# A new order of all engines and PSUM banks in the third stage of a decoder kernel: value projections between the head products and the scores

## The chip, the cores and the metric

The kernel runs on one core of one Trainium2 chip. The metric is the device time of the whole program in microseconds, as the median of several executions. Numbers of the trace come from one further execution under the hardware profiler.

## The reference

The input is 64 sequences of 64 tokens with 128 features. Three stages follow each other, each with a residual addition: a self-attention, a cross-attention, and a stack of six layers, which the change touches. Cut to what matters, one of the six layers is:

```python
qkv = shift_tokens(x) @ Wqkv[i]                 # 128 -> 3 * 1024, 16 heads of 64
q, k = l2norm(q) * q_scale[i], l2norm(k) * k_scale[i]
q, k = rotary(q), rotary(k)                     # k with the inverse scale
sim = where(mask, -max, (q @ k.T) * 8.0)        # local window, causal
out = softmax(sim) @ v
x = out @ Wo[i] + x
xn = layernorm(shift_tokens(x)) * g + b
a, gate = split(xn @ W1[i] + b1[i])             # 2 * 341
x = a * gelu(gate) @ W2[i] + b2[i] + x
```

All of it is float32.

## The kernel before

A tile holds two sequences, 128 tokens on 128 partitions, so there are 32 tiles a layer and N = 192 tiles in six layers. The third stage is the function `local`. Every engine runs its own program, written out as one loop over i from 0 to N + LAST (LAST = 8), and in each pass it takes one step of each kind for tiles of different age: `queries(i, 0)` of the newest tile, `scores(i - 1)` of the one before, `ff_out(i - 8)` of the oldest. The order of the calls in the five loops, and which of the eight PSUM banks each result uses, are written out in the program; nothing reorders them at run time. An engine executes its own list strictly in that order. Between engines there are counting semaphores: `Counted` translates "this half of tile t is done" into a count, from the order in which the halves are written, and `wait_ge` holds the engine until the count is there. A bank is used by several results in turn, so some waits are only there to keep a bank from being overwritten too early.

What a tile goes through, with the lines under which the profile shows it:

- TensorE: `input_turned` (a transpose, `ident,ystat`, L1008), `queries` and `keys` (products with the weights WA, L1032), `queries_turned` and `keys_turned` (four transposes each of R, L1008), `values` (eight products, L1083), `scores` (mask L1098, 64 small products L1103), `probs_turned` (transposes of P, L1008), `head_outputs` (64 small products of V and PT, L1144), `out_projection` (L1160), `normal_turned` (transpose of xn), `ff_in` (L1128), `ff_out` (L1024).
- ScalarE: squares of queries and keys from their banks (L1219), copies out of the banks (L1194), exponentials (L1232), the normalised tile (L1242), and the gates.
- VectorE: rotation of queries and keys from the banks into R (L1319), sums of squares, a seed for the inverse root (L1344), the maximum of the scores and its subtraction, sums of rows and their inverse (L1373), the two additions to Y (L1294 attention, L1300 feed-forward), the gating.
- GpSimd: `queries_added` and `keys_added` are DMAs from R to R that add the second half of the rotation (L1419 and L1424, issued from GpSimd's queue), `inverse_lengths` is twelve short steps (L1465 to L1472), `keys_scaled` (L1432), `scores_scaled` (L1438), `probs_scaled` (L1444), `inverse_deviation` (L1450 to L1454). `keys_scaled` waits for the landing of the keys' DMA, and by the order of the loop everything below it waits too.
- SyncE issues the loads: the tile's shifted input, the shifted tile for the feed-forward part, and the weights of the next layer.

R, which the rotation writes and the DMAs, the scaling and the transposes read, exists once for queries and once for keys; P, qT, kT and PT exist twice.

GpSimd's loop before is this one:

```python
for i in range(N + LAST + 1):
    queries_added(i)
    probs_scaled(i - 3, 0)
    keys_added(i)
    inverse_lengths(i)
    keys_scaled(i, 0)
    keys_scaled(i, 1)
    scores_scaled(i - 1, 1)
    probs_scaled(i - 2, 1)
    scores_scaled(i - 1, 0)
    inverse_deviation(i - 4)
```

## Time and profile before

| | |
|---|---|
| median of three executions | 3528.43 us (3526.76 to 3532.59) |
| the profiled execution | 3525.89 us, its span 3524.1 us |
| granted TensorE clock | 0.993 of full speed |
| TensorE products | 3377.9 us busy, 96% of the span, 49,605 of them |
| TensorE weight loads | 2495.3 us, 71%, 49,605 of them |
| VectorE | 2811.5 us, 80% |
| ScalarE | 2792.7 us, 79% |
| GpSimd | 2475.5 us, 70% |
| the chain that ended last | TensorE 78% of the span, "issue" 2%, each other engine at most 1% |

Busy time counts how long an engine's instructions ran, overlapping ones once. A busy TensorE is not one at its peak. "issue" in the chain or in a wait is time in which the engine waited for nothing that the profile shows. The third stage begins near 566 us, and its 192 tiles enter between 569.4 and 3446.0 us.

### The profile page before, as it was taken

To read this page: it belongs to the slowest core of one execution; us is meant where nothing else is said; L and a number is where in the kernel's file an instruction comes from. 1 tells how busy PE (TensorE), PEld (TensorE's weight loads), DVE (VectorE), ACT (ScalarE), POOL (GpSimd) and SP (SyncE) were. 2 spreads that over 40 slices of the span, in tenths; PEclk is the share of its full clock that TensorE was granted. 3 is DMA by queue.
4 is the path that set the end of the run, shared out by engine and by line. 5 is a ranking of instruction groups with operands and counts; after the bars stand their busy time and mean duration, and the time that the engine had idled before them with its cause. 6 is when DMAs were issued, how large, how long until landed. Compare 5 with 4: busy or idle time off the path is not lost.

```text
span 3524.1 us, 120975 instructions
## 1 busy us (share of the span) xinstructions
PE 3377.9 (96%) x49605; PEld 2495.3 (71%) x49605; DVE 2811.5 (80%) x5297; ACT 2792.7 (79%) x5522; POOL 2475.5 (70%) x4812
## 2 busy tenths in 40 slices
PE   8989997999999999999999999999999999999997
PEld 5778774677777777777777777777777777777776
DVE  6834445888888888888888888888888888888885
ACT  5756664688888888888888888888888888888885
POOL 5622224777777777777777777777777777777774
PEclk9999998999999999999999999999999999999999
DMA  3000002444444444444444444444444444444441
GB/s 101 3 10 8 9 6 50 92 82 82 82 81 89 95 82 82 80 88 97 82 82 82 83 90 93 82 82 80 90 96 83 82 82 88 78 85 83 88 85 39
DMA packets 200382, 260.17 MB, mean 74 GB/s; under 512 B 123161, under 2 KB 145438, under 8 KB 199838
## 3 DMA queue, kind: packets, MB, share of 16 engines
q0 software_dynamic: 55296, 201.35, 30.4%
q1 hardware_dynamic: 143820, 50.88, 5.8%
q8 instruction: 400, 6.55, 0.8%
q14 instruction: 144, 1.18, 0.1%
q10 hardware_dynamic: 722, 0.21, 0.0%
HBM read 23.95 MB, written 2.10 MB: 7 GB/s over the span
## 4 chain that ended last, share of the span: by engine, by line
PE 78%; issue 2%; DVE 1%; POOL 1%; DMA 1%; ACT 0%; SPq 0%; POOLq 0%; DVEq 0%
PE bank L1032 18%; PE bank L1008 16%; PE bank L1083 10%; PE bank L1160 10%; PE bank L1128 7%; PE bank L1144 6%; PE bank L1103 5%; PE bank L1024 3%; PE bank L1098 2%; DVE R L1319 1%; DMA R<-R 1%; POOL R L1432 0%; POOL P L1444 0%; DVE ss L1332 0%; POOL P L1438 0%
## 5 line engine op out<-in xcount | busy, mean ns | idle before, releaser
L1319 DVE TENSOR_TENSOR R<-bank,tables 128x1024 f32<-128x1024 f32 x768 | 903.6, 1218 | 167.5 <-ACT sq L1219 127.4
L1032 PE MATMUL bank<-WA,xcT 128*128 128x512 f32 x1536 | 757.6, 596 | 1.8 <-ACT xcT L1194 1.8
L1008 PEld LDWEIGHTS bank<-ident,R 128*128 128x128 f32 x3072 | 371.6, 141 | 307.0 <-issue 299.9
L1444 POOL TENSOR_TENSOR P<-P,inv_sum 128x512 f32<-128x512 f32 x384 | 458.2, 1193 | 13.1 <-DVE inv_sum L1373 12.1
L1332 DVE TENSOR_REDUCE ss<-sq 128x16 f32<-128x1024 f32 x384 | 460.3, 1199 | 0.0
L1219 ACT ACTIVATE sq<-bank 128x512 f32<-128x512 f32 x768 | 438.2, 595 | 23.9 <-PE bank L1032 23.5
L1432 POOL TENSOR_TENSOR R<-R,rn 128x512 f32<-128x512 f32 x384 | 392.3, 1042 | 88.1 <-DMA R<-R 73.4
L1008 PE MATMUL bank<-ident,R 128*128 128x128 f32 x3072 | 429.8, 273 | 3.3 <-POOL R L1432 2.4
L1438 POOL TENSOR_TENSOR P<-P,rn 128x512 f32<-128x512 f32 x384 | 402.5, 1048 | 2.1 <-DVE P L1361 2.1
L1160 PE MATMUL bank<-WO,OT 128*128 128x128 f32 x3072 | 386.4, 279 | 1.7 <-ACT OT L1194 1.7
L1083 PE MATMUL bank<-WV,xcT 128*64 128x512 f32 x1536 | 376.0, 606 | 3.2 <-DVE R L1319 2.9
L1160 PEld LDWEIGHTS bank<-WO,OT 128*128 128x128 f32 x3072 | 357.4, 192 | 5.3 <-ACT OT L1194 1.9
L1194 ACT ACTIVATE PT<-bank 128x512 f32<-128x512 f32 x384 | 230.2, 599 | 146.8 <-PE bank L1008 146.8
L1194 ACT ACTIVATE kT<-bank 128x512 f32<-128x512 f32 x384 | 233.3, 608 | 133.6 <-PE bank L1008 133.6
L1032 PEld LDWEIGHTS bank<-WA,xcT 128*128 128x128 f32 x1536 | 248.6, 192 | 97.2 <-issue 94.3
L1128 PE MATMUL bank<-xnT,W 128*128 128x128 f32 (+1 forms) x2304 | 287.5, 275 | 0.0
L1194 ACT ACTIVATE V<-bank 128x512 f32<-128x512 f32 x384 | 230.5, 600 | 71.9 <-PE bank L1083 71.9
L1008 PEld LDWEIGHTS bank<-ident,P 128*128 128x128 f32 x1536 | 170.8, 141 | 164.1 <-issue 155.1
L1103 PE MATMUL bank<-kT,qT 64*64 64x64 f32 x12288 | 234.5, 219 | 54.6 <-issue 54.6
L1103 PEld LDWEIGHTS bank<-kT,qT 64*64 64x64 f32 x12288 | 229.7, 135 | 71.0 <-issue 61.9
L1361 DVE TENSOR_TENSOR P<-bank,mx 128x512 f32<-128x512 f32 x384 | 263.2, 686 | 6.7
L1128 PEld LDWEIGHTS bank<-xnT,W 128*128 128x128 f32 (+1 forms) x2304 | 264.8, 180 | 0.1
(154 smaller groups left out, 7082.5 us busy)
## 6 DMA issues: line engine op xcount, KB each, us to landing
R<-R POOLq DMA_DIRECT2D x384, 512.0 KB, 5.3
WA<-in_wqkv SPq DMA_DIRECT2D x24, 256.0 KB, 2.8
ystat<-Y SPq DMA_DIRECT2D x192, 32.0 KB
ystat<-Y SPq DMA_DIRECT2D x384, 15.8 KB
ys<-Y SPq DMA_DIRECT2D x192, 32.0 KB
ys<-Y SPq DMA_DIRECT2D x384, 15.8 KB
WV<-in_wqkv SPq DMA_DIRECT2D x6, 512.0 KB, 5.9
WO<-in_wo SPq DMA_DIRECT2D x6, 512.0 KB, 4.3
```

Source lines behind the costliest of these rows:

```text
L1008: return nc.tensor.transpose(dst, src, m.ident[:, :])
L1032: mm(b[QK_BANK[n, half]][:, :], m.xsT[:, t % 2, :], cols[:, half, :, :], start=True, stop=True)\
L1083: last = mm(V_BANK[bb][64 * e:64 * e + 64, :], m.xsT[:, t % 2, bb * 64:bb * 64 + 64], cols[:, e, :, :], start=True, stop=True)
L1103: last = mm(S_BANK[a][64 * bb:64 * bb + 64, hp * 64:(hp + 1) * 64], m.qT[head, t % 2, at:at + 64], m.kT[head, t % 2, at:at + 64], start=Fa ...
L1128: last = mm(FF_BANK[c][0:rows, side * 128:(side + 1) * 128], m.W1[:, off + at:off + at + rows], m.xnT[:, t % 2, :], start=True, stop=True)
L1160: last = mm(OUT[:, 0:128], m.OT[:, t % 2, at:at + 128], wo[:, c * 128:(c + 1) * 128], start=(c == 0), stop=(c == PAIRS - 1))
L1194: return nc.scalar.activation(dst, src, ACT.Copy)
L1219: nc.scalar.activation(by_half[:, half, :, :], b[QK_BANK[n, half]][:, :].rearrange("p (h d) -> p h d", d=32), ACT.Square)\
L1319: tt(both, src.unsqueeze(1).to_broadcast([128, 2, 16, 32]), tab.unsqueeze(2).to_broadcast([128, 2, 16, 32]), ALU.mult).then_inc(s.rotated. ...
L1332: nc.vector.tensor_reduce(m.ss[:, t % 2, 16 * n:16 * n + 16], m.sq[:, n, :].rearrange("p (h d) -> p h d", d=HD), AX.X, ALU.add)\
L1438: tt(part, part, wide(m.rn[:, t % 4, a:16:2]), ALU.mult).then_inc(s.scaled.sem, 1)
L1444: tt(part, part, wide(m.inv_sum[:, t % 2, 8 * a:8 * a + 8]), ALU.mult).then_inc(s.normal.sem, 1)
```

## The change

The instructions and what they compute stay the same; each engine's list of calls within a pass, the banks, and the waits that go with them are new.

- TensorE: `values` of tile i moves from behind `scores` to between `head_outputs` and `scores`. The two `queries` products now follow each other, the transposes of queries, the transpose of xn (a pass later than before) and `ff_out` follow them, and the transposes of keys and of the probabilities' half 1 stand between and behind the two `keys` products.
- ScalarE: the same calls in a new order; the first exponential stands among the squares, `normal_out` and `normalised` work on tiles one pass older.
- VectorE: the rotation of keys takes half 1 first; maximum and subtraction alternate; `statistics` stands near the end of the pass, and `ff_added` last, for the tile i - 7 in place of i - 8 at the second place.
- GpSimd: `probs_scaled` of half 0 moves from between the two DMAs (tile i - 3) to behind `keys_scaled` (tile i - 2); the scalings of keys, half 1 first, are no longer next to each other; `inverse_deviation` is for a tile one pass older.
- Banks: all have new numbers but those that happen to agree.
- Waits: each step waits for what frees its new bank. New on TensorE: `queries(t, 0)` for the subtraction of the scores' half 0, `queries_turned` for that of half 1, `keys(t, 1)` for the feed-forward addition, `values` for the copy of the turned keys, `head_outputs` for the rotation of the queries' half 1, `probs_turned` for the rotation of keys and the copy of queries, `scores` for the copy of the head outputs.

The diff, cut: most unchanged lines are left out, and those of the five loops stand.

```diff
--- before.py
+++ after.py
@@ -898,11 +898,11 @@
-    QK_BANK = {(QUERIES, 0): 3, (QUERIES, 1): 6, (KEYS, 0): 1, (KEYS, 1): 2}
-    TURNED_IN, TURNED_OUT = b[4], b[6]
-    KT_BANK, QT_BANK, V_BANK = (b[7], b[0]), (b[7], b[4]), (b[1], b[4])
-    S_BANK, PT_BANK, PV_BANK = (b[5], b[6]), (b[0], b[0]), (b[4], b[3])
-    OUT, FF_BANK, FF_OUT = b[0], (b[2], b[1], b[7]), b[5]
+    QK_BANK = {(QUERIES, 0): 1, (QUERIES, 1): 2, (KEYS, 0): 4, (KEYS, 1): 6}
+    TURNED_IN, TURNED_OUT = b[2], b[7]
+    KT_BANK, QT_BANK, V_BANK = (b[0], b[5]), (b[3], b[0]), (b[0], b[5])
+    S_BANK, PT_BANK, PV_BANK = (b[1], b[3]), (b[4], b[3]), (b[1], b[2])
+    OUT, FF_BANK, FF_OUT = b[7], (b[0], b[5], b[6]), b[6]
@@ -911,15 +911,15 @@
-    s.qk, s.squared, s.rotated = counted("qk", *four), counted("squared", *four), counted("rotated", *four)
+    s.qk, s.squared, s.rotated = counted("qk", *four), counted("squared", *four), counted("rotated", (QUERIES, 0), (QUERIES, 1), (KEYS, 1), (KEYS, 0))
...
-    s.q_added, s.k_added, s.k_scaled = sem("local_q_added"), sem("local_k_added"), counted("k_scaled", 0, 1)
+    s.q_added, s.k_added, s.k_scaled = sem("local_q_added"), sem("local_k_added"), counted("k_scaled", 1, 0)
...
-    s.q_turned, s.q_copied = counted("q_turned", 1, 0), counted("q_copied", 0, 1)
+    s.q_turned, s.q_copied = counted("q_turned", 0, 1), counted("q_copied", 0, 1)
...
-    s.scores, s.mx, s.less = sem("local_scores"), counted("mx", 0, 1), counted("less", 1, 0)
-    s.scaled, s.probs, s.row_sum = counted("scaled", 1, 0), counted("probs", 0, 1), counted("row_sum", 0, 1)
-    s.inverse, s.normal = counted("inverse", 0, 1), counted("normal", 1, 0)
+    s.scores, s.mx, s.less = sem("local_scores"), counted("mx", 0, 1), counted("less", 0, 1)
+    s.scaled, s.probs, s.row_sum = counted("scaled", 0, 1), counted("probs", 0, 1), counted("row_sum", 1, 0)
+    s.inverse, s.normal = counted("inverse", 1, 0), counted("normal", 1, 0)
@@ -1010,7 +1010,9 @@
-                    at_least(pe, s.v_copied.sem, s.v_copied.upto(1, t))
+                    at_least(pe, s.o_copied.sem, s.o_copied.upto(1, t - 4))
+                    if t < 5:
+                        at_least(pe, s.rotated.sem, s.rotated.upto((QUERIES, 1), t))
@@ -1037,23 +1039,22 @@
-                    else:
-                        at_least(pe, s.less.sem, s.less.upto(1, t - 1))
+                        at_least(pe, s.less.sem, s.less.upto(0, t - 1))
...
-                    if half == 1 and t < 2:
-                        at_least(pe, s.rotated.sem, s.rotated.upto((KEYS, 1), t))
+                    if half == 1:
+                        at_least(pe, s.y, t - 7)
+                    elif t < 2:
+                        at_least(pe, s.rotated.sem, s.rotated.upto((KEYS, 0), t))
...
-                        pe.wait_ge(s.q_copied.sem, s.q_copied.upto(0, t + 1))
-                    elif t < 8:
-                        at_least(pe, s.y1, t - 3)
+                        pe.wait_ge(s.q_copied.sem, s.q_copied.upto(1, t + 1))
@@ -1063,9 +1064,9 @@
+                        at_least(pe, s.less.sem, s.less.upto(1, t))
+                    else:
...
-                    elif t == N - 1:
-                        pe.wait_ge(s.v_copied.sem, s.v_copied.upto(1, t + 1))
@@ -1075,10 +1076,8 @@
-                        pe.wait_ge(s.rotated.sem, s.rotated.upto((KEYS, 0), t + 1))
+                        at_least(pe, s.k_copied.sem, s.k_copied.upto(0, t))
...
-                    else:
-                        at_least(pe, s.o_copied.sem, s.o_copied.upto(0, t - 3))
@@ -1088,10 +1087,10 @@
-                    at_least(pe, s.xn_copied, t - 4)
-                    at_least(pe, s.y, t - 6)
-                    if t < 6:
-                        pe.wait_ge(s.rotated.sem, s.rotated.upto((QUERIES, 1), t + 2))
+                    at_least(pe, s.o_copied.sem, s.o_copied.upto(0, t - 2))
+                    if t < 5:
+                        pe.wait_ge(s.rotated.sem, s.rotated.upto((QUERIES, 0), t + 2))
+                        at_least(pe, s.p_copied.sem, s.p_copied.upto(1, t - 1))
@@ -1109,9 +1108,9 @@
-                        pe.wait_ge(s.p_copied.sem, s.p_copied.upto(1, t + 1))
+                        pe.wait_ge(s.rotated.sem, s.rotated.upto((KEYS, 0), min(t + 4, N)))
...
-                        pe.wait_ge(s.k_copied.sem, s.k_copied.upto(1, min(t + 3, N)))
+                        pe.wait_ge(s.q_copied.sem, s.q_copied.upto(0, min(t + 3, N)))
@@ -1121,8 +1120,9 @@
-                    pe.wait_ge(s.v_copied.sem, s.v_copied.upto(0, min(t + 8, N)))
-                    pe.wait_ge(s.rotated.sem, s.rotated.upto((KEYS, 1), min(t + 8, N)))
+                    pe.wait_ge(s.v_copied.sem, s.v_copied.upto(1, min(t + 8, N)))
+                    if t >= N - 8:
+                        pe.wait_ge(s.y, t)
@@ -1132,10 +1132,8 @@
-                    pe.wait_ge(s.v_copied.sem, s.v_copied.upto(0, t + 1))
-                    pe.wait_ge(s.q_copied.sem, s.q_copied.upto(1, min(t + 4, N)))
-                    if t < 2:
-                        pe.wait_ge(s.rotated.sem, s.rotated.upto((QUERIES, 0), t + 5))
+                    pe.wait_ge(s.v_copied.sem, s.v_copied.upto(1, t + 1))
+                    pe.wait_ge(s.rotated.sem, s.rotated.upto((QUERIES, 1), min(t + 5, N)))
@@ -1149,11 +1147,8 @@
-                    pe.wait_ge(s.o_copied.sem, s.o_copied.upto(0, t + 1))
...
-                    if t >= N - 6:
-                        pe.wait_ge(s.p_copied.sem, s.p_copied.upto(0, min(t + 2, N)))
@@ -1164,27 +1159,27 @@
             def normal_turned(t):
                 if exists(t):
                     pe.wait_ge(s.xn, t + 1)
-                    pe.wait_ge(s.rotated.sem, s.rotated.upto((QUERIES, 1), min(t + 7, N)))
+                    pe.wait_ge(s.y1, min(t + 3, N))
                     turned(TURNED_OUT[:, 0:128], m.xn[:, t % 2, :]).then_inc(s.xn_turned, 1)
 
             for i in range(N + LAST + 1):
                 input_turned(i)
                 out_projection(i - 5)
                 queries(i, 0)
-                queries_turned(i - 1, 1)
                 queries(i, 1)
                 queries_turned(i - 1, 0)
+                queries_turned(i - 1, 1)
+                normal_turned(i - 7)
+                ff_out(i - 8)
                 keys(i, 0)
+                keys_turned(i - 1, 1)
+                probs_turned(i - 3, 1)
                 keys(i, 1)
-                keys_turned(i - 1, 1)
                 keys_turned(i - 1, 0)
-                ff_out(i - 8)
-                probs_turned(i - 3, 1)
-                normal_turned(i - 6)
                 head_outputs(i - 4)
-                scores(i - 1)
                 values(i, 0)
                 values(i, 1)
+                scores(i - 1)
                 probs_turned(i - 3, 0)
                 ff_in(i - 7)
 
@@ -1265,23 +1260,23 @@
                 input_out(i)
                 gates(i - 8)
                 squares(i, QUERIES, 0)
+                queries_out(i - 1, 0)
                 squares(i, QUERIES, 1)
-                queries_out(i - 1, 0)
+                exponents(i - 2, 0)
                 squares(i, KEYS, 0)
+                queries_out(i - 1, 1)
                 keys_out(i - 1, 1)
-                queries_out(i - 1, 1)
                 squares(i, KEYS, 1)
                 keys_out(i - 1, 0)
-                normal_out(i - 6)
-                exponents(i - 2, 0)
+                normal_out(i - 7)
+                probs_out(i - 3, 1)
                 outputs_out(i - 4, 0)
-                probs_out(i - 3, 1)
+                values_out(i, 0)
+                normalised(i - 6)
+                values_out(i, 1)
+                outputs_out(i - 4, 1)
                 exponents(i - 2, 1)
-                normalised(i - 5)
-                outputs_out(i - 4, 1)
-                values_out(i, 0)
                 probs_out(i - 3, 0)
-                values_out(i, 1)
 
         @block.vector
         def _(dve):
@@ -1307,11 +1302,10 @@
-                    if half == 0:
-                        if n == QUERIES:
-                            at_least(dve, s.q_turned.sem, s.q_turned.upto(0, t))
-                        elif t < 9:
-                            at_least(dve, s.k_turned.sem, s.k_turned.upto(0, t))
+                    if n == KEYS and half == 1:
+                        at_least(dve, s.k_turned.sem, s.k_turned.upto(0, t))
+                    elif n == QUERIES and half == 0 and t < 9:
+                        at_least(dve, s.q_turned.sem, s.q_turned.upto(1, t))
@@ -1385,23 +1379,23 @@
             for i in range(N + LAST + 1):
                 rotary(i, QUERIES, 0)
                 rotary(i, QUERIES, 1)
-                statistics(i - 5)
                 squares_summed(i, QUERIES)
-                ff_added(i - 8)
+                rotary(i, KEYS, 1)
                 rotary(i, KEYS, 0)
-                rotary(i, KEYS, 1)
                 squares_summed(i, KEYS)
                 seeded(i)
                 maximum(i - 1, 0)
+                less_maximum(i - 1, 0)
+                row_sums(i - 2, 1)
+                row_sums(i - 2, 0)
                 maximum(i - 1, 1)
                 less_maximum(i - 1, 1)
-                row_sums(i - 2, 0)
-                less_maximum(i - 1, 0)
+                inverse_sums(i - 2, 1)
+                gated(i - 7)
+                attention_added(i - 4)
+                statistics(i - 5)
                 inverse_sums(i - 2, 0)
-                attention_added(i - 4)
-                gated(i - 7)
-                row_sums(i - 2, 1)
-                inverse_sums(i - 2, 1)
+                ff_added(i - 7)
 
         @block.gpsimd
         def _(pool):
@@ -1420,12 +1414,12 @@
-                    pool.wait_ge(s.rotated.sem, s.rotated.upto((KEYS, 1), t + 1))
+                    pool.wait_ge(s.rotated.sem, s.rotated.upto((KEYS, 0), t + 1))
...
-                    if j == 0:
+                    if j == 1:
@@ -1474,15 +1468,15 @@
 
             for i in range(N + LAST + 1):
                 queries_added(i)
-                probs_scaled(i - 3, 0)
                 keys_added(i)
                 inverse_lengths(i)
+                keys_scaled(i, 1)
+                scores_scaled(i - 1, 0)
+                probs_scaled(i - 2, 1)
                 keys_scaled(i, 0)
-                keys_scaled(i, 1)
+                probs_scaled(i - 2, 0)
                 scores_scaled(i - 1, 1)
-                probs_scaled(i - 2, 1)
-                scores_scaled(i - 1, 0)
-                inverse_deviation(i - 4)
+                inverse_deviation(i - 5)
 
 
 # ---- launch: one core; inputs and outputs as the reference has them ----

```

## Rows read from the trace of the kernel before

**Rows 1.** Groups of instructions, 709 to 3430 us: name, shapes, count | busy us, mean ns | idle before.
```profile
L1008 PE MATMUL bank<-ident,ystat 128*128 128x128 f32 x180 | 53.9, 300 | 0.0
```
**Rows 2.** TensorE in order of time, one undisturbed cycle: start us, us, line, operation, count.
```profile
2057.91 0.30 PE L1008 MATMUL bank<-ident,ystat 128*128 128x128 f32 x1
...
2065.75 0.60 PE L1008 MATMUL bank<-ident,P 128*128 128x128 f32 x4
2066.19 0.27 PE L1008 MATMUL bank<-ident,xn 128*128 128x128 f32 x1
2066.40 1.16 PE L1144 MATMUL bank<-PT,V 64*64 64x64 f32 x64
2067.51 0.41 PE L1098 MATMUL bank<-causalb,identb 64*64 64x512 bf16 x4
2067.72 1.13 PE L1103 MATMUL bank<-kT,qT 64*64 64x64 f32 x64
2068.78 1.94 PE L1083 MATMUL bank<-WV,xcT 128*64 128x512 f32 x8
2070.65 0.66 PE L1008 MATMUL bank<-ident,P 128*128 128x128 f32 x4
...
2072.57 0.30 PE L1008 MATMUL bank<-ident,ystat 128*128 128x128 f32 x1
```
**Rows 3.** Who waited for whom, 709 to 3430 us: us in total, times, longest.
```profile
POOL R L1432 <- DMA R<-R: 68.2, 99, 2.8
...
PE bank L1103 <- issue: 53.0, 58, 1.5
...
POOL P L1444 <- DVE inv_sum L1373: 2.2, 8, 0.5
```
**Rows 4.** The chain that ended last, around one gap: start us, us, what.
```profile
2089.38 0.86 PE bank L1032 x2
2090.24 0.44 PE bank L1008 x4
...
2097.24 0.43 PE bank L1103 x26
2097.66 0.97 issue
```
**Rows 5.** The page's DMA queues: packets, MB, share of 16 engines.
```profile
q8 instruction: 400, 6.55, 0.8%
```
**Rows 6.** GpSimd in order of time, three cycles; what ended an idle time in brackets.
```profile
1310.45 0.94 POOL L1419 DMA_DIRECT2D R<-R  x1
1311.12 1.35 POOL L1444 TENSOR_TENSOR P<-P,inv_sum 128x512 f32<-128x512 f32 x1
1313.04 0.88 POOL L1424 DMA_DIRECT2D R<-R  x1 [0.56 <-DVE R L1319]
...
1319.26 2.04 POOL L1432 TENSOR_TENSOR R<-R,rn 128x512 f32<-128x512 f32 x2 [0.89 <-DMA R<-R]
1321.26 1.05 POOL L1438 TENSOR_TENSOR P<-P,rn 128x512 f32<-128x512 f32 x1
1322.26 1.04 POOL L1444 TENSOR_TENSOR P<-P,inv_sum 128x512 f32<-128x512 f32 x1
1323.26 1.05 POOL L1438 TENSOR_TENSOR P<-P,rn 128x512 f32<-128x512 f32 x1
...
1325.59 0.94 POOL L1419 DMA_DIRECT2D R<-R  x1
...
1327.69 0.88 POOL L1424 DMA_DIRECT2D R<-R  x1
...
1334.31 2.04 POOL L1432 TENSOR_TENSOR R<-R,rn 128x512 f32<-128x512 f32 x2 [1.29 <-DMA R<-R]
...
1340.64 0.94 POOL L1419 DMA_DIRECT2D R<-R  x1
...
1348.07 2.04 POOL L1432 TENSOR_TENSOR R<-R,rn 128x512 f32<-128x512 f32 x2 [0.27 <-DMA R<-R]
```
**Rows 7.** VectorE in order of time, feed-forward addition and the rotations behind it.
```profile
2066.55 0.28 DVE L1300 TENSOR_TENSOR Y<-Y,bank 128x128 f32<-128x128 f32 x1
2066.75 2.35 DVE L1319 TENSOR_TENSOR R<-bank,tables 128x1024 f32<-128x1024 f32 x2
```
**Rows 8.** Tile R with GpSimd's instructions, 709 to 3430 us: its DMAs, issue to landing.
```profile
DMA to landing us min/median/max: 4.5/5.3/8.0
```

## Prediction

> **What bounds the kernel now.** I read the page first: TensorE is busy 96% of the span, VectorE and ScalarE some 80%, GpSimd 70%, so only TensorE looks like a bound. Then I asked how even the third stage runs. The transpose of an input tile, one in each pass of the loop, stands 180 times in 2,721 us, which is 15.12 us a cycle [rows 1]. An undisturbed cycle takes 2072.57 - 2057.91 = 14.66 us on TensorE, with no gap in it [rows 2]. So 0.46 us a cycle is lost. The list of waits names the larger part: TensorE waits inside the scores (L1103) for "issue", that is for nothing that the profile shows, 58 times, 53.0 us in all [rows 3]. The chain shows one of them: 26 products, 0.97 us of nothing, then the rest [rows 4]. With these waits TensorE executes the two densest runs of the program back to back: 64 head products from 2066.40, the mask at 2067.51, 64 products of the scores until 2068.78, some 270 instructions in 2.4 us [rows 2]. The instruction queue of the page brought 400 packets, 6.55 MB, 16 KB each [rows 5]; at 64 bytes an instruction that is 102,400, near the 99,210 products and loads of TensorE on the page and its waits. One packet then feeds 256 instructions, fewer than the two runs together hold. I take the gap for a late packet.
>
> The Trainium skill speaks against this reading (Runtime: NRT & Kernel Launch, section Instruction fetch mechanics): refills come in blocks of 256 instructions, and the cost of crossing into a new one is mostly hidden by the issue floor. The block size agrees with the packets here, "mostly hidden" doesn't agree with 53.0 us. By that rule the spreading would gain nothing.
>
> The last view is GpSimd alone, in order of time, and it decides my forecast. In each cycle GpSimd issues an accumulating DMA for the queries (L1419), one for the keys (L1424), computes the inverse lengths, and must then wait until the keys' DMA has landed before it scales the keys (L1432); it waited for that in 99 of 180 cycles [rows 3]. After that point come two scalings of keys, three steps on the probabilities and the inverse deviation, then the next queries' DMA. In the cycle from 1310.45: the queries' DMA is issued at 1310.45, scaling of keys begins at 1319.26 after a wait, the next queries' DMA is issued at 1325.59 [rows 6]. That is a closed loop on one engine in order: 8.81 us for the two transfers, 6.33 us of work. The next loops measure 1334.31 - 1325.59 = 8.72 and again 6.33, so 15.1 us each, already more than TensorE's 14.66; others are shorter and the slack between the engines evens it out. The keys' transfer gains nothing from an earlier issue: issued 2.59 us behind the queries' it took 6.22, issued 2.10 behind it took 6.62, as if it stood behind the first [rows 6].
>
> **The change part by part.**
>
> TensorE's order. The same instructions run. The eight products of values (1.87 us, 2068.78 to 2070.65 [rows 2]) now stand between head products and scores. 132 pairs within 2.4 us become two runs of at most 1.3 us with 1.87 us of slow work between them. If my reading of the gap is right it closes: the gap was 0.97 us [rows 4], on average 53.0/58 = 0.91, and 1.87 us more are available. Worth up to 53 us if TensorE is the bound, nothing if it isn't. Lower bound nothing (the gap only moves).
>
> The array changes its tiling once more: full to quarter to column tiles to quarter to full. A change costs here 0.10 us: the single transpose ahead of the head products takes 0.21 us (2066.19 to 2066.40), a transpose within its run 0.44/4 = 0.11 [rows 2]. One more is +0.1 us a cycle, 19 us if TensorE binds; but the head products no longer run straight into the mask, where the rows can't tell how much of 1.11 us was a join. I take 0, between -0.1 and +0.1. The Trainium skill (TensorEngine Tiling (Array Packing), section Key Properties) says that a change of tiling mode drains the array; by it the upper end would be taken, 14.76 us.
>
> Banks and waits. New waits on TensorE: queries and their transposes on the subtracted scores, keys half 1 on the feed-forward sum, head products on the queries' rotation, values on the copied keys. Behind each stands all of TensorE. The tightest that I find is that of the head products on the rotation of the newest queries. Between feed-forward product and head products TensorE has both key products (0.86 us each) and three groups of four transposes (0.44 each [rows 4]), 3.04 us. In that time VectorE, whose list ends with the feed-forward addition and begins anew with the queries, has the addition, 0.20 us to the next start, and two rotations, 2.35 us [rows 7]: 2.55, and 0.5 to spare less the signals. I take 0, and up to 0.2 us a cycle if it is late.
>
> VectorE and ScalarE. No instruction is added or dropped. VectorE is busy 80% of the span by the page, so the new wait for the feed-forward product at the end of its pass has some 2 us of idle time to lie in; queued behind it are the next rotations, counted above. Statistics and normalisation come a pass later, and `LAST` stays 8: nothing in the steady part.
>
> GpSimd's order. This is the term that counts. The normalisation of the probabilities' half 0 stood between the two DMA issues (1311.12 [rows 6]), beside the transfers, where GpSimd would have waited anyway. It now stands behind the keys' landing with the other five. Between scaling and the next queries' DMA there are now six steps and the deviation, 6.33 us plus one step. That step measures 1323.26 - 1322.26 = 1.00 us where no DMA is written beside it [rows 6]. So 7.33 us. A wait inside it I leave out: for the inverse sums it waited 2.2 us in 180 cycles [rows 3], and both are now formed before the pass in which they are used ends. That makes 7.33 a lower bound of this part.
>
> The two transfers remain. From the queries' issue to the keys' scaling the sample has 8.81, 8.72, and 7.43 (1348.07 - 1340.64) us [rows 6]. Over 180 cycles the median landing is 5.3 us behind an issue, least 4.5, most 8.0 [rows 8]; with 2.59 us between the issues and 0.07 to start, 7.96. I take 8.1, nearer to the median of all than to the three. The ends are 7.43 and 8.8.
>
> **The sum.** GpSimd's loop becomes 8.1 + 7.33 = 15.43 us, above TensorE's 14.66 and above today's mean of 15.12. It binds every cycle, since queries' DMA, landing and steps follow each other on one engine, and nothing can run ahead of it. +0.31 us a cycle, from about the fifth tile to the last of 192, 187 cycles: +58 us. TensorE's closed gap is worth nothing then: it idles some 0.8 us a cycle ahead of the transposes of probabilities or keys. Filling and draining I take as unchanged: the drain has the same chain per tile, up to 5 us either way. The profiled execution took 3525.9 us (span 3524.1 and 1.8 around it), the median of the runs is 2.5 us above it. 3528.4 + 58 = 3586.
>
> **The rivals.**
> - **TensorE stays the bound and the gap closes** (faster). The loop on GpSimd would have to be short: 7.43 + 7.33 = 14.76 us, which needs every pair of transfers at the sample's best. A cycle of 14.8 gives (14.8 - 15.12) x 187 = -60 us: 3469. For it: if packets of instructions are what delays the transfers, their new times may miss them. Against it: the two other loops of the sample take 8.7 and more. It decides below 7.79 us of landing (7.79 + 7.33 = 15.12). Chance 0.15.
> - **Break-even.** Landing 7.75 to 7.83 us, the gain eaten exactly: 3522 to 3535, 3528. Chance 0.10.
> - **Worse than the forecast.** Both DMAs are issued closer together and the transfers meet more of other traffic, 8.8 us as in the sample: 16.13 us a cycle, +189 us. Partly so, 8.5 us: +133 us, 3661. Chance 0.10.
> - **The gap doesn't close**, since it has another cause. Then it lies in TensorE's new idle time, and the time is the forecast's. That is part of the forecast.
>
> **How the numbers follow.** Forecast 0.65, with 7.9 to 8.4 us of landing: 15.23 to 15.73, +21 to +114 us, 3549 to 3642. The range reaches down to break-even and some way into the faster rival, 3510, and up to 3642. Within 0.2% (7 us, about what a measurement of this kernel can tell from no change): 0.10. Faster: 0.15. Slower: 0.65 + 0.10 = 0.75.
>
> **What would show it.** Right: GpSimd waits for the keys' DMA in nearly all cycles, 0.5 us and more each; 7.3 us from that scaling to the next queries' DMA in every cycle, without a wait; TensorE idle ahead of the transposes of probabilities, released by GpSimd; the row "L1103 <- issue" nearly gone. Wrong: a cycle on TensorE of 14.7 without gaps, which would mean that the transfers land within 7.4 us of the queries' issue; or TensorE waiting for VectorE's rotation ahead of the head products, which would mean that my placing of VectorE was off.

## The result and the profile after

The changed kernel takes 3649.35 us (median of four runs, 3645.76 to 3653.86), beside 3530.51 us for the kernel before on the same chip: a ratio of 1.0333, 95% interval 1.0317 to 1.0348. It is slower by 119 us; 58 were forecast. The profiled execution took 3645.8 us, against 3525.9 before, so the traces carry the whole difference.

The page of the changed kernel: busy time of each engine, the chain that ended last, and two groups of instructions (busy, mean ns of one, idle before them and its releaser). Lines are numbered anew: the DMAs are L1413 (queries) and L1418 (keys), scaling of keys L1426, scores' products L1102.

```profile
PE 3358.6 (92%) x49605; PEld 2446.6 (67%) x49605; DVE 2827.0 (78%) x5297; ACT 2824.3 (78%) x5522; POOL 2466.6 (68%) x4812
...
DMA 39%; POOL 38%; PE 3%; DVE 2%; issue 2%; ACT 0%; SPq 0%; DVEq 0%; POOLq 0%
...
L1426 POOL TENSOR_TENSOR R<-R,rn 128x512 f32<-128x512 f32 x384 | 400.4, 1043 | 453.3 <-DMA R<-R 452.9
...
L1008 PE MATMUL bank<-ident,P 128*128 128x128 f32 x1536 | 252.7, 287 | 195.6 <-POOL P L1438 195.1
```

TensorE is still the busiest engine, 92%, and yet it has 3% of the chain. The chain goes round a loop: GpSimd, the DMAs R<-R, GpSimd again. Busy shares don't show such a bound; the chain does.

The list of waits of the changed kernel in 712 to 3556 us, the even part of the stage (us in total, times, longest):

```profile
POOL R L1426 <- DMA R<-R: 433.7, 180, 4.8
...
PEld bank L1008 <- POOL P L1438: 224.2, 179, 1.6
...
PE bank L1008 <- POOL P L1438: 182.0, 161, 1.4
```

Beside [rows 3]: GpSimd's wait for the keys' DMA was 68.2 us in 99 cycles and is now 433.7 in 180. The scores' products no longer wait for "issue" (53.0 us before, no such row for TensorE now). In its place TensorE waits for the normalised probabilities, 182.0 us.

GpSimd in order of time through one loop (start, duration, line; the twelve short steps in between left out):

```profile
2020.23 0.94 POOL L1413 DMA_DIRECT2D R<-R  x1
2020.88 1.19 POOL L1418 DMA_DIRECT2D R<-R  x1
...
2029.06 1.04 POOL L1426 TENSOR_TENSOR R<-R,rn 128x512 f32<-128x512 f32 x1 [2.88 <-DMA R<-R]
2030.06 1.05 POOL L1432 TENSOR_TENSOR P<-P,rn 128x512 f32<-128x512 f32 x1
2031.06 1.04 POOL L1438 TENSOR_TENSOR P<-P,inv_sum 128x512 f32<-128x512 f32 x1
...
2036.38 0.94 POOL L1413 DMA_DIRECT2D R<-R  x1
```

From the keys' scaling to the next queries' issue it takes 2036.38 - 2029.06 = 7.32 us: the forecast's 7.33. From the queries' issue to the scaling it takes 2029.06 - 2020.23 = 8.83 us. Taken over the 180 cycles of the trace, tile 10 to 189: 7.35 us of work, and 8.43 us to the scaling (8.36 to the keys' landing, 0.07 to start), where 8.1 was forecast. The sum is 15.78 us, the mean cycle.

So the loop was forecast and the loop is there. What was missed is 0.33 us of landing, 60 us in all. In the trace of before the same stretch has a mean of 8.03 us to landing. It isn't one value with a small spread. In the changed kernel 114 of 182 cycles have 8.4 to 8.8 us, 28 less than 7.6, and only 3 lie between 8.0 and 8.4; before, they spread from 7.3 to 8.8, with 57 below 7.6 and 46 from 8.4 to 8.8. The experiments ask what decides between short and long.

### The profile page after: what moved, and what is told of

Read it like the earlier page. It is cut to its first block, busy times and chain, and to the rows that moved or that the text cites. A ratio compares the mean times of both kernels' runs of the same rounds, so it can differ in the third digit from the quotient of the medians.

```text
span 3644.0 us, 120785 instructions
## 1 busy us (share of the span) xinstructions
PE 3358.6 (92%) x49605; PEld 2446.6 (67%) x49605; DVE 2827.0 (78%) x5297; ACT 2824.3 (78%) x5522; POOL 2466.6 (68%) x4812
## 4 chain that ended last, share of the span: by engine, by line
DMA 39%; POOL 38%; PE 3%; DVE 2%; issue 2%; ACT 0%; SPq 0%; DVEq 0%; POOLq 0%
DMA R<-R 39%; POOL R L1426 10%; POOL P L1432 10%; POOL P L1438 10%; POOL R L1413 3%; POOL rstd L1446 3%; POOL nmr L1448 1%; DVE R L1313 1%; POOL vare L1444 1%; PE bank L1034 1%; PE bank L1008 1%; PE bank L1128 0%; PE bank L1155 0%; DVE ss L1326 0%; PE bank L1026 0%
## 5 line engine op out<-in xcount | busy, mean ns | idle before, releaser
L1426 POOL TENSOR_TENSOR R<-R,rn 128x512 f32<-128x512 f32 x384 | 400.4, 1043 | 453.3 <-DMA R<-R 452.9
L1008 PEld LDWEIGHTS bank<-ident,R 128*128 128x128 f32 x3072 | 362.3, 141 | 341.0 <-issue 174.7
L1214 ACT ACTIVATE sq<-bank 128x512 f32<-128x512 f32 x768 | 452.2, 589 | 111.3 <-PE bank L1034 110.5
L1008 PE MATMUL bank<-ident,P 128*128 128x128 f32 x1536 | 252.7, 287 | 195.6 <-POOL P L1438 195.1
L1438 POOL TENSOR_TENSOR P<-P,inv_sum 128x512 f32<-128x512 f32 x384 | 400.6, 1043 | 6.3 <-DVE inv_sum L1367 6.3
L1227 ACT ACTIVATE P<-P 128x512 f32<-128x512 f32 x384 | 243.5, 634 | 205.6 <-POOL P L1432 205.2
L1155 PE MATMUL bank<-WO,OT 128*128 128x128 f32 x3072 | 374.7, 276 | 0.6 <-ACT OT L1189 0.5
L1008 PEld LDWEIGHTS bank<-ident,P 128*128 128x128 f32 x1536 | 161.6, 141 | 252.5 <-POOL P L1438 239.6
L1295 DVE TENSOR_TENSOR Y<-Y,bank 128x128 f32<-128x128 f32 x192 | 55.3, 288 | 298.3 <-PE bank L1026 298.3
L1347 DVE TENSOR_REDUCE mx<-bank 128x8 f32<-128x512 f32 x384 | 263.4, 686 | 7.3 <-PE bank L1102 7.1
```

The costliest lines, as they stand in the source:

```text
L1008: return nc.tensor.transpose(dst, src, m.ident[:, :])
L1155: last = mm(OUT[:, 0:128], m.OT[:, t % 2, at:at + 128], wo[:, c * 128:(c + 1) * 128], start=(c == 0), stop=(c == PAIRS - 1))
L1214: nc.scalar.activation(by_half[:, half, :, :], b[QK_BANK[n, half]][:, :].rearrange("p (h d) -> p h d", d=32), ACT.Square)\
L1426: tt(part, part, wide(m.rn[:, t % 4, 16 + 8 * j:24 + 8 * j]), ALU.mult).then_inc(s.k_scaled.sem, 1)
L1438: tt(part, part, wide(m.inv_sum[:, t % 2, 8 * a:8 * a + 8]), ALU.mult).then_inc(s.normal.sem, 1)
```

## The experiments

### Undoing GpSimd's part, and making it alone

```diff
                 queries_added(i)
+                probs_scaled(i - 3, 0)
                 keys_added(i)
...
                 keys_scaled(i, 0)
-                probs_scaled(i - 2, 0)
```

> The changed kernel with one line of it undone: GpSimd's normalisation of the probabilities' half 0 stands again between the two DMA issues, one pass later, as before the change. TensorE, VectorE, ScalarE and all banks stay as changed. Theory (GpSimd's closed loop sets the time): the work between the landing of the keys' DMA and the next queries' DMA falls from 7.33 to 6.33 us, the landing stays near 8.1 to 8.4, so the loop takes 14.4 to 14.8 us and TensorE's 14.6 becomes the bound again; with the gap in the scores closed the time falls below the kernel before: 3445 to 3480 us. Rival 1 (the new orders of TensorE, VectorE or the banks lose the time): stays at 3640 to 3650. Rival 2 (the landing grows to 8.8 once the step lies between the issues, as some cycles of the kernel before show): 15.1 us a cycle, about 3530, the kernel before again.

3494.6 us (3489.4 to 3503.7), ratio to before 0.9909 (0.9893 to 0.9925). One moved step is worth 155 us; rival 1 falls, and rival 2 would have needed 8.8 us of landing and 3530 us. But it isn't at TensorE's bound either: chain and waits (712 to 3380 us) of this kernel are

```profile
POOL 32%; DMA 29%; PE 15%; DVE 5%; issue 2%; ACT 0%; SPq 0%; POOLq 0%; DVEq 0%
...
POOL R L1426 <- DMA R<-R: 250.1, 173, 4.5
```

The work is 6.35 us, as it should be, but the keys land 8.54 us behind the queries' issue: 14.97 us a cycle. The expectation was low by 15 us or more, for the same reason as the forecast: the landing was taken from another kernel. The kernel is faster than the one before although its landing is the longest so far.

The other way round, the kernel before with GpSimd's part alone:

```diff
                 queries_added(i)
-                probs_scaled(i - 3, 0)
                 keys_added(i)
...
                 scores_scaled(i - 1, 0)
+                probs_scaled(i - 2, 0)
                 inverse_deviation(i - 4)
```

> The kernel before with GpSimd's part of the change alone: the normalisation of the probabilities' half 0 leaves its place between the two DMA issues and goes, a pass earlier, behind the scaling of the scores' half 0 at the end of the order. Theory (GpSimd's loop): 7.33 us of work behind the keys' landing; with a landing of 8.1 us, as forecast, 15.43 us a cycle and 3586 us; with 8.43, as the changed kernel shows, 15.76 us and 3645. Which of the two it is tells whether the longer landing comes with the two issues standing closer together (then it is here too) or with something else of the change. Rival (the loop isn't the bound): 3530 and below, no change.

3551.0 us (3540.2 to 3558.1), ratio 1.0073 (1.0056 to 1.0089). Neither value: 7.35 us of work as expected, but a landing of 7.77 us, 15.20 a cycle. Here too the issues stand 0.67 us apart in 76 of 182 cycles, and in these the landing has the same mean as in the others, 7.75 and 7.78 us; the shortest ones got shorter, 7.18 us instead of 7.35. That the issues stand close together therefore doesn't lengthen the landing. The two halves of the change make a square:

| | GpSimd's order before | GpSimd's order changed |
|---|---|---|
| all else before | landing 8.03, 3528 us | 7.77, 3551 us (+23) |
| all else changed | 8.54, 3495 us (-34) | 8.36, 3649 us (+119) |

The parts alone come to -11 us, together to +119. And the landing follows the other engines' orders, in both columns: it is longer by half a microsecond where they run their new ones, though the DMAs and their data are the same.

### The two transfers in a row

```diff
-pool.dma_start(m.R[:, QUERIES, 0, :], m.R[:, QUERIES, 1, :], accum_op=ALU.add)
+pool.dma_start(m.R[:, QUERIES, 0, 0:512], m.R[:, QUERIES, 1, 0:512], accum_op=ALU.add)
```

> The changed kernel with the queries' accumulating DMA cut to half of its columns (the rotated halves of the other queries aren't added, so the output is wrong). Theory (the two transfers go one after the other and stand in GpSimd's loop): the queries' part takes 1.37 us instead of 2.74, the keys land 1.37 us earlier, 8.43 becomes 7.06, the loop takes 14.4 us, TensorE binds at 14.6 to 14.7 us: 3435 to 3455 us. Rival (the transfers run side by side and only the keys' own time counts, or the loop isn't the bound): 3640 to 3650 us.

3436.7 us (3436.6 to 3436.8), ratio 0.9742 (0.9722 to 0.9761). Half of the queries' transfer is 1.17 us of landing (8.36 to 7.19 us; 1.37 expected), and the chain is TensorE's:

```profile
PE 51%; DMA 12%; POOL 12%; DVE 6%; issue 2%; ACT 0%; SPq 0%; POOLq 0%
```

The time is within the expected range, the rival's 3640 to 3650 us is far off. The keys' data do stand behind the queries', and GpSimd's loop is the bound of the changed kernel.

### Packets of TensorE's instructions

Every packet of TensorE's instruction queue (16 KB, 399 of them in this program) was set against the queries' issue of its cycle. In all four kernels of the square, cycles with a packet that starts 2 to 6 us behind that issue (called hit below) have a landing of 8.5 to 8.7 us on the mean. The other cycles have 7.7 to 7.9, in the kernel with GpSimd's part undone 8.2 (36 cycles), and those with no packet at all between issue and landing 7.3 to 7.5, though these are few: 10, 53, 18 and 2 cycles in the order of the counts that follow. The limits of 2 and 6 us were set from these same traces. How many cycles are hit differs most, of 182: 43 before, 17 with GpSimd's part alone, 108 in the changed kernel, 146 with GpSimd's part undone. That is the order of their landings (8.03, 7.77, 8.36, 8.54). It is only a coincidence in the traces so far. The first try to act on it leaves out most of TensorE's small products:

```diff
-                    for hp in range(PAIRS):
+                    for hp in (PAIRS - 1,):
...
-                    for j in range(4):
-                        for bb in range(2):
-                            for e, a in ((0, 0), (1, 1), (0, 1), (1, 0)):
+                    for e, a in ((0, 0), (1, 1), (0, 1), (1, 0)):
...
+                        last = mm(PV_BANK[e][head, :], m.V[keys, t % 4, a * 64:a * 64 + 64],
+                                  m.PT[keys, t % 2, a * 512:a * 512 + 512], start=True, stop=True)
```

> The changed kernel with most of TensorE's small products left out: of the scores only the mask and the last of the eight groups, and the 32 head products are replaced by four wide ones, which compute something else. TensorE then has less than half of its instructions in a cycle. GpSimd's order and all DMAs stay. Theory (packets of TensorE's instructions delay the accumulating DMAs): windows from the queries' issue to the keys' landing hold a packet less often, the mean landing falls from 8.43 to about 7.6 us and the time to 3480 to 3530 us. Rival (the closeness of the issues, or traffic of other queues, lengthens the landing): the landing stays at 8.3 to 8.5 us and the time within 10 us of 3645.

3541.1 us (3540.2 to 3547.7), ratio 1.0042 (1.0026 to 1.0058): 108 us less than the changed kernel, with 206 instead of 430 instructions a cycle, 231 packets instead of 399 on the page, 34 cycles hit, and a landing of 7.83 us (expected 7.6; 3480 to 3530 us was some 10 us too low). It speaks for packets, but less work on TensorE might act in another way. The clean test keeps the work and moves only the packets. It starts from the kernel with few products, puts four of the eight groups of scores back and transposes each input tile twice. With exactly 256 instructions a cycle one packet comes per cycle, always at the same place, and transposes ahead of the first cycle choose which:

```diff
+                    for _ in range(33 if t == 0 else 1):
+                        turned(TURNED_IN[:, 0:128], m.ystat[:, t % 2, :])
                     turned(TURNED_IN[:, 0:128], m.ystat[:, t % 2, :]).then_inc(s.x_turned, 1)
...
-                    for hp in (PAIRS - 1,):
+                    for hp in range(4, PAIRS):
```

The diff is against the kernel with few products. 33 is the kernel shifted by 64 instructions; the others have 1, 65 and 97.

> Four kernels that differ in one number only. All have the changed kernel's orders; of the computation they leave out the first four of the eight groups of scores and replace the 32 head products by four wide ones, and they transpose each input tile twice, so that TensorE executes exactly 256 instructions in a cycle (430 records in the changed kernel, less 64, less 112, plus 2). One packet of 256 instructions then comes in each cycle, always at the same place of the cycle. Here that place is where it falls by itself; in the others it is moved by transposes that are repeated once, ahead of the first cycle (32, 64 and 96 of them, 64, 128 and 192 instructions). Theory (a packet that starts 2 to 6 us behind the queries' issue makes the keys land at 8.65 us, one outside that stretch leaves 7.2 to 7.5): the four kernels differ though each does the same work in each cycle; those whose packet falls inside take 8.65 + 7.33 + 0.07 = 16.05 us a cycle and 3680 to 3700 us, those outside 14.6 to 14.9 and 3430 to 3480. Rival (the landing has another cause and packets only go along with it): all four within 15 us of each other, and near the 3541 us of the kernel with few products.

> As the kernel without shift, with 64 more instructions ahead of the first cycle. Theory: the packet comes a quarter of 256 instructions earlier in each cycle, some 2 to 6 us; at least one of the four kernels lies wholly inside the stretch of 2 to 6 us and at least one outside, 200 us apart. Rival: all four within 15 us.

> As the kernel without shift, with 128 more instructions ahead of the first cycle, half of the 256: the packet at the other side of the cycle. Theory: 3430 to 3480 us if it falls outside, 3680 to 3700 if inside. Rival: all four within 15 us.

> As the kernel without shift, with 192 more instructions ahead of the first cycle. Theory: 3430 to 3480 us if the packet falls outside, 3680 to 3700 if inside. Rival: all four within 15 us.

| shift | us (one run) | cycles hit, of 182 | landing, us |
|---|---|---|---|
| 0 | 3466.5 | 0 | 7.42 |
| 64 | 3708.3 | 167 | 8.68 |
| 128 | 3539.2 | 2 | 7.76 |
| 192 | 3560.0 | 4 | 7.83 |

242 us between two kernels that do the same work in each cycle. Shift 0 fell into the range expected for a packet outside, shift 64 is 8 us above the one for a packet inside. Shifts 128 and 192 missed both ranges. GpSimd in order of time, shift 0 and then shift 64; here L1411 is the queries' issue and L1424 the scaling of keys:

```profile
2011.73 0.94 POOL L1411 DMA_DIRECT2D R<-R  x1
...
2019.01 1.04 POOL L1424 TENSOR_TENSOR R<-R,rn 128x512 f32<-128x512 f32 x1 [1.32 <-DMA R<-R]
...
2026.35 0.94 POOL L1411 DMA_DIRECT2D R<-R  x1
```

```profile
2018.38 0.97 POOL L1411 DMA_DIRECT2D R<-R  x1
...
2027.16 1.04 POOL L1424 TENSOR_TENSOR R<-R,rn 128x512 f32<-128x512 f32 x1 [2.81 <-DMA R<-R]
...
2034.48 0.94 POOL L1411 DMA_DIRECT2D R<-R  x1
```

And the queues in the stretch of 2 to 6 us behind those issues (packets, MB, share of the 16 DMA engines), 2013.73 to 2017.73 of shift 0, then 2020.38 to 2024.38 of shift 64:

```profile
q0 software_dynamic: 208, 0.79, 103.7%
```

```profile
q0 software_dynamic: 206, 0.78, 103.2%
q8 instruction: 1, 0.02, 1.5%
```

One packet of 1.5% in a stretch in which the accumulating DMAs fill all the engines, and the scaling of keys begins 8.78 - 7.28 = 1.50 us later; on the mean of all cycles the landing is 1.26 us later. The work behind them is the same, 7.34 and 7.32 us. The rival (packets only go along with the landing, all four within 15 us) falls, since in the cycles nothing but their place differs. Each shift was run once, so a difference of a few us between them says nothing. The other two shifts are less clean: hardly a cycle is hit, and yet they take 7.8 us. In both the packet starts at the same place, 0.9 us (median) behind the queries' issue, where it seems to cost less, 0.3 to 0.4 us beside shift 0; that part is read from the traces, not tested.

That the changed kernel is slow by this and not by where its instructions happen to begin:

```diff
+                    for _ in range(32 if t == 0 else 0):
+                        turned(TURNED_IN[:, 0:128], m.ystat[:, t % 2, :])
```

> The changed kernel, whole, with 32 transposes repeated ahead of the first cycle, 64 instructions. With 430 instructions in a cycle the packets move through all places of the cycle, 168 packets in 100 cycles. Theory: a shift of the start changes nothing that lasts; the share of cycles whose packet falls 2 to 6 us behind the queries' issue stays near 60%, the time within 10 us of 3645 to 3650. Rival (the changed kernel is slow by the luck of where its instructions begin): it moves by 20 us or more, in either direction.

3646.0 us (3642.2 and 3649.7), ratio 1.0342 (1.0302 to 1.0381), 103 cycles hit. As expected: with 430 instructions a cycle this shift of the start averages out.

### TensorE's gap, and what its new order is worth

```diff
-                    for j in range(4):
+                    for j in (2, 3):
```

in the head products of the kernel before.

> The kernel before with half of the head products left out (the heads of two of four column groups). TensorE executes 64 instructions less ahead of the scores. Theory (the gap in the scores is a packet of 256 instructions that comes late behind the dense run of head products and scores): the wait of the scores' products for nothing that the profile shows, 58 times and 53 us, falls to under 10 us. Rival (the gap belongs to the scores alone, whatever runs ahead of them): it stays at 45 us or more. The time may stay near 3500, since GpSimd's loop of some 15.1 us is still there.

3473.7 us, one run, 14.81 us a cycle: GpSimd's loop didn't hold it at the 15.1 us that the expectation named. The wait for nothing falls from 53.0 us in 58 cycles [rows 3] (51.9 in 57 over 712 to 3380 us) to (712 to 3380 us):

```profile
PE bank L1103 <- issue: 10.6, 22, 1.0
...
PE bank L1098 <- ACT xnT L1209: 77.6, 179, 0.6
```

just above the "under 10" expected, far from the rival's 45. The second row shows that the run changes more than the count of instructions: TensorE now also waits 0.43 us a cycle for ScalarE ahead of the mask, and that pause may have helped as well. In the trace of before, moreover, a packet starts 1.4 us (median) before TensorE stops inside the scores, and TensorE goes on 2.5 us behind that start, in 60 cycles. From the first product of the scores to the values it takes 2.21 us in 62 cycles, instead of 1.06.

The last pair was to take GpSimd's loop out of both kernels' way, by moving the deviation's three steps in between the DMA issues:

```diff
                 queries_added(i)
+                inverse_deviation(i - 6)
+                probs_scaled(i - 3, 0)
                 keys_added(i)
...
-                probs_scaled(i - 2, 0)
                 scores_scaled(i - 1, 1)
-                inverse_deviation(i - 5)
```

> The changed kernel with GpSimd's order alone changed: the normalisation of the probabilities' half 0 back between the two DMA issues (as in the run with it alone), and the three steps of the inverse deviation moved there too, from the end of a pass to behind the next queries' issue. GpSimd's work between the keys' landing and the next queries' issue is then 7.33 less 1.00 less about 1.19 (the deviation's steps), 5.15 us. Theory (GpSimd's loop bound both this kernel and the run with half 0 back): with a landing of 8.55 us the loop takes 13.8 us, TensorE binds at its undisturbed 14.45 us a cycle: 3430 to 3450 us, the fastest so far with the whole computation. Rival (in the run with half 0 back it was TensorE's waits for others that kept the time at 3495, or the later deviation delays the normalised tiles): 3480 to 3500 us.

3419.3 us (3412.0 to 3428.1), ratio to before 0.9700 (0.9666 to 0.9735). With the whole computation it is 3% below the kernel before and 6% below the changed one, better than the 3430 to 3450 expected. Its chain, two transposes of an input tile one cycle apart, and its wait for the keys' DMA (712 to 3380 us):

```profile
PE 68%; POOL 5%; DMA 5%; DVE 4%; issue 1%; ACT 0%; SPq 0%; POOLq 0%; DVEq 0%
```

```profile
2003.57 0.27 PE L1008 MATMUL bank<-ident,ystat 128*128 128x128 f32 x1
...
2011.43 0.60 PE L1008 MATMUL bank<-ident,R 128*128 128x128 f32 x4
2011.96 1.16 PE L1142 MATMUL bank<-PT,V 64*64 64x64 f32 x64
2013.05 1.94 PE L1082 MATMUL bank<-WV,xcT 128*64 128x512 f32 x8
2014.92 0.41 PE L1097 MATMUL bank<-causalb,identb 64*64 64x512 bf16 x4
2015.16 1.10 PE L1102 MATMUL bank<-kT,qT 64*64 64x64 f32 x64
2016.19 0.66 PE L1008 MATMUL bank<-ident,P 128*128 128x128 f32 x4
...
2018.01 0.27 PE L1008 MATMUL bank<-ident,ystat 128*128 128x128 f32 x1
```

```profile
POOL R L1426 <- DMA R<-R: 59.7, 72, 2.7
```

The cycle shown is 14.44 us without a gap; over the stage the mean is 14.59, and the wait for nothing inside the scores comes once, 0.3 us. The landing isn't short here: 8.85 us on the mean, 8.81 in the 125 cycles with a packet 2 to 6 us behind the issue and 8.92 in the other 57. Only 5.5 us of work and waits stand behind it. The same relief for the kernel before:

```diff
                 queries_added(i)
+                inverse_deviation(i - 5)
                 probs_scaled(i - 3, 0)
                 keys_added(i)
...
-                inverse_deviation(i - 4)
```

> The kernel before with the inverse deviation moved between its two DMA issues, so that GpSimd's loop (8.0 to 8.4 us and 5.15) stays below TensorE's cycle. TensorE's old order stays, with its gap in the scores. Theory: TensorE binds alone, 14.66 us and the gap, 53 us in 180 cycles, 0.3 us: 14.96 us a cycle, 3495 to 3510 us. The difference to the changed kernel with the same relief (3430 to 3450) is then what the new order of TensorE is worth by itself, 50 to 65 us. Rival (the gap costs nothing and all of the loss above 14.66 us was GpSimd's): 3440 to 3455 us, no difference to the other.

3557.1 us (3550.3 to 3562.9), ratio 1.0089 (1.0061 to 1.0116): a miss on both counts, slower than without the relief. TensorE does bind it alone, but its gap has grown (the chain, and the wait in 712 to 3380 us):

```profile
PE 79%; issue 2%; DVE 1%; POOL 1%; DMA 0%; ACT 0%; SPq 0%; POOLq 0%; DVEq 0%
...
PE bank L1103 <- issue: 66.4, 55, 1.9
```

1.21 us each, where it was 0.91. The scores with a gap take 2.54 us in 58 cycles, instead of 2.21 in 62, and here 130 of the 182 cycles have a packet 2 to 6 us behind the queries' issue. The landing is 9.03 us, the longest of all, again with little difference between these cycles (9.13) and the others (8.78). A packet that is late for TensorE and lies in the transfers may be slowed by them in turn; the trace fits that, no run tested it. What the pair does show: with the deviation's steps in the same place, the rest of the new plan is worth 3557 - 3419 = 138 us, far more than the 53 us that the forecast allowed TensorE's order. The two kernels differ in the orders of all engines and in the banks, so not all of it need be TensorE's; its closed gap, (2.54 - 1.06) x 58 = 86 us, and its shorter undisturbed cycle, 40 us (below), come near it.

## Why the prediction was right or wrong

**GpSimd's loop as the new bound: right.** It waits for the keys' DMA in 180 of 180 cycles, TensorE idles ahead of the transposes of probabilities, and one moved step back gives 155 us.

**The work in the loop, 7.33 us: right**, 7.35 on the mean, without a wait inside.

**The two transfers, 8.1 us: this term was mis-sized**, and it carries the whole error. It measured 8.43 us; 0.33 x 187 = 62 us, and 58 + 62 = 120 are the 120 us of the two profiled executions. The step that failed is to have taken the landing from the trace of before as if it belonged to the transfer. For that kernel 8.1 us was right: its mean is 8.03 and 0.07 to start, though it came out partly by luck, since the median of 5.3 us [rows 8] is over the DMAs of queries and keys together, and that of the keys alone is 5.51. But the landing goes by how often a packet of TensorE's instructions falls into it, 43 cycles of 182 before and 108 after, and that share is set by the orders that the change rewrites. An estimate of the size: hit and other cycles of the changed kernel are 8.67 - 7.92 = 0.75 us apart, times 65/182 more cycles hit gives 0.27 of the 0.33 us. That a packet's place alone moves the landing is shown on the kernel with fewer products; for the changed kernel itself its share is read from the trace. The forecast named packets only in its faster rival ("their new times may miss them"); their new times hit.

In the cycle shown above, TensorE begins the scores 0.85 us behind the queries' issue (first row, of the order of time), and a packet falls into the stretch of 2 to 6 us (second row, of the queues in 2022.23 to 2026.23):

```profile
2021.08 1.10 PE L1102 MATMUL bank<-kT,qT 64*64 64x64 f32 x64
```

```profile
q8 instruction: 1, 0.02, 1.5%
```

The rival "worse than the forecast" gave closeness of the issues as its reason; that was wrong, since issued closer the shortest landings are shorter (7.18 against 7.35 us).

**The new waits on TensorE: right to cost them at nothing.** The tightest, the head products on VectorE's rotation, is 2.2 us in 4 cycles (same list of waits as above):

```profile
PE bank L1142 <- DVE R L1313: 2.2, 4, 0.6
```

**TensorE's gap: right that it closes, and that it is a late packet**; half of the products, with the pause that comes with them, leave a fifth of it. Too small in size: the profile's waits show 53 us, but the scores' blocks lost (2.21 - 1.06) x 62 = 71 us of the 0.46 x 180 = 83 us above the undisturbed cycle.

**One more change of tiling, -0.1 to +0.1 us: the sum 0 was near, the whole cycle was not.** Head products, values, mask and scores take 1.092 + 1.867 + 0.240 + 1.036 = 4.24 us apart (the fastest kernel), against 1.112 + 0.215 + 1.056 + 1.868 = 4.25 joined (before). The Trainium skill (TensorEngine Tiling (Array Packing), section Key Properties) says that a change of tiling mode drains the array; a cost of the added change isn't to be seen in that sum. The 0.10 us ahead of the head products that the prediction read off is there in both orders: the transpose of the normalised tile stood there before (0.20 us, now 0.11), and four transposes of keys stand there now and take 0.53 us (2011.43 to 2011.96 in the rows above), where the same four take 0.44 elsewhere. But the undisturbed cycle fell from 14.66 to 14.44 us, 40 us over the stage, in the output projection (1.85 to 1.79) and the feed-forward products (1.43 to 1.33) for the most part. Why these became shorter wasn't looked into. The forecast had no term for it; in the changed kernel it is hidden behind GpSimd.

**Why break-even or a gain was thought of and didn't come.** The gain is real: 34 us with one line changed back, 106 us with the deviation moved too. It was turned into waits, 182 us of TensorE's ahead of the transposes of probabilities.

The rule on instruction refills that the prediction set against the gap (the Trainium skill, Runtime: NRT & Kernel Launch, section Instruction fetch mechanics) holds for the block of 256 instructions: that count a cycle pins the packets to one place. That their cost is mostly hidden doesn't hold for the dense runs before, where it is 71 us on TensorE, nor for a loop of DMAs, where it is up to 242 us between two alignments.

## What to carry to other kernels

Look for closed loops across engines and DMAs, not only for the busiest engine: an instruction in the shadow of a transfer can be nearly free, and the same instruction behind its landing lengthens every pass once the loop is the bound, here by 0.81 us for a step of 1.00 (15.78 and 14.97 us a cycle). Before moving work out of such a shadow, add up the loop; here one step of 1.00 us made the gain of a whole new plan into a loss, and going the other way, with four steps in the shadow, won 3%. The shadow is no gift by itself: where TensorE was the bound, three more steps in it made the kernel before 1% slower. Take a transfer's time from the old trace only together with what crosses it there, since a new order of another engine moves that too.

## What the runs showed of the hardware

- One 16 KB packet of TensorE's instructions that starts 2 to 6 us behind the queries' issue delays the landing of two accumulating DMAs of 512 KB by about 1.3 us (7.42 and 8.68 us on the mean of shifts 0 and 64), though it is 1.5% of the DMA engines' time there. How it does so isn't shown. With the deviation's steps between the two issues the landing is 8.8 to 9.1 us with such a packet and 8.8 to 8.9 without; why the packet makes no clear difference there is open.
- The alignment of a program's instructions to blocks of 256 can be worth 7% (3466.5 and 3708.3 us) when the count per cycle divides evenly, and nothing (3646.0 and 3649.4 us) when it doesn't.
- Of two accumulating DMAs on GpSimd's queue, the second one's data wait for the first's; 0.65 or 2.5 us between the issues make 0.17 us of difference to the shortest landings of the pair (7.18 and 7.35 us).
- With the deviation's short steps running between the issues, the queries' data took 4.07 us to pass in the kernel before and 3.49 in the fastest kernel, against 2.82 without them. That wasn't looked into.
